# A two-layer decoder on one NeuronCore: first weights are loaded during the layer norm, an attention block's opening is reordered, and its last denominators and outputs are made in another way

## The reference

```python
x = x + L0_attn(_layernorm(x), ...)            # 16 heads of 64, keys: the 1024 tokens
x = x + L0_xattn(_layernorm(x), ctx_768, ...)  # 16 heads of 64, keys: 6404 context rows of 96
x = x + L0_ffn(_layernorm(x), ...)             # 8 experts, top 2, and a shared MLP; 512 hidden, gelu
x = x + L1_attn(_layernorm(x), ...)            # 16 heads of 8, rotary
x = x + L1_xattn(_layernorm(x), ctx_768, ...)  # 8 heads of 64, 6404 context rows
x = x + L1_ffn(_layernorm(x), ...)             # 8 experts, top 2, 512 hidden, relu

# one cross attention
sim  = jnp.einsum('bhid,bhjd->bhij', q, k) * SCALE
attn = jax.nn.softmax(sim, axis=-1)
out  = jnp.einsum('bhij,bhjd->bhid', attn, v)   # then heads side by side @ Wo + bo
```

## Time and profile before

| | |
|---|---|
| median of 3 runs | 4294.48 us (4294.39 to 4295.44) |
| the profiled execution's own time | 4298.41 us |
| its span, first to last instruction | 4296.6 us |
| mean granted TensorE clock, share of full | 0.961 |
| busy share of the span | PE 94%, PEld 50%, DVE 62%, ACT 42%, POOL 66% |
| DMA | 23.92 MB, mean 6 GB/s |
| L404, POOL's adds in c0 and c1 | x1176, 2482.9 us busy |
| L569, DVE's maxima in c0 and c1 | x1156, 1391.5 us busy |
| L473, ACT's exponentials in c0 and c1 | x1224, 1192.9 us busy |
| L785, PE's products in c0 and c1 | x4896 (two records each), 1179.9 us busy |

### The profile page before, as it was taken

How to read it: one execution, slowest core, us unless ns; L and a number is a source line. 1 busy time by engine, 2 the same in 40 slices (tenths; PEclk the granted TensorE clock), 3 DMA queues, 4 the chain that set the end, 5 groups by cost and what they waited for, 6 DMA issues and landing times. The chain is left out here.

```text
span 4296.6 us, 71788 instructions
## 1 busy us (share of the span) xinstructions
PE 4020.1 (94%) x26404; PEld 2141.9 (50%) x26404; DVE 2685.1 (62%) x3375; ACT 1813.3 (42%) x2105; POOL 2825.2 (66%) x1350
## 2 busy tenths in 40 slices
PE   6999699999999999999999997889899999999969
PEld 3444355554545555555555544633355554555537
DVE  5766767667676676766667622387666666667432
ACT  2444144444444444444444442256244444444433
POOL 3667187878887787877878891000077888878940
PEclk9999899999999999999999998989599999999979
DMA  1000000000000000000000000100000000000001
GB/s 36 6 6 2 5 2 2 2 2 2 2 2 3 2 2 2 2 3 2 2 1 1 2 1 27 35 1 1 4 2 2 2 2 2 2 1 2 1 13 32
DMA packets 25454, 23.92 MB, mean 6 GB/s; under 512 B 6321, under 2 KB 19106, under 8 KB 25122
## 3 DMA queue, kind: packets, MB, share of 16 engines
q1 hardware_dynamic: 23666, 17.05, 1.4%
q10 hardware_dynamic: 1456, 2.46, 0.2%
HBM read 18.97 MB, written 0.52 MB: 5 GB/s over the span
## 5 line engine op out<-in xcount | busy, mean ns | idle before, releaser
L404 POOL TENSOR_TENSOR c_SUM<-c_SUM,c_PR 128x896 f32<-128x896 f32 (+1 forms) x1176 | 2482.9, 2111 | 452.6 <-ACT c_PR L473 360.3
L569 DVE TENSOR_REDUCE c_MX<-c_XB 128x2 f32<-128x1024 f32 (+2 forms) x1156 | 1391.5, 1204 | 849.5 <-PE c_XB L735 848.9
L473 ACT ACTIVATE c_PR<-c_S 128x1024 f32<-128x1024 f32 (+1 forms) x1224 | 1192.9, 1023 | 1628.6 <-PE c_S L769 1553.0
L785 PE MATMUL c_O<-c_PR,c_V 128*64 128x512 f32 (+1 forms) x4896 | 1179.9, 600 | 1.3 <-ACT c_PR L473 1.3
L785 PEld LDWEIGHTS c_O<-c_PR,c_V 128*64 128x64 f32 (+1 forms) x4896 | 316.4, 136 | 542.2 <-issue 382.4
L769 PE MATMUL c_S<-c_SH,c_ONE 64*128 64x512 f32 x2448 | 486.4, 392 | 0.0
L735 PE MATMUL c_XB<-c_KHM,c_QH 64*128 64x512 f32 x1632 | 371.8, 449 | 26.4 <-DVE c_MX L569 20.2
L769 PE MATMUL c_S<-c_QH,c_KHM 64*128 64x512 f32 x1728 | 350.2, 401 | 0.1
L769 PE MATMUL c_S<-c_QH,c_KLM 64*128 64x512 f32 x1728 | 346.0, 396 | 0.0
L769 PE MATMUL c_S<-c_QL,c_KHM 64*128 64x512 f32 x1728 | 345.9, 395 | 0.0
L735 PEld LDWEIGHTS c_XB<-c_KHM,c_QH 64*128 64x128 f32 x1632 | 155.5, 186 | 378.8 <-DVE c_MX L569 206.7
(11 more groups left out here) (264 smaller groups left out, 4541.4 us busy)
## 6 DMA issues: line engine op xcount, KB each, us to landing
f_W<-in_L_w SPq DMA_DIRECT2D x34, 256.0 KB, 2.7
CTX<-in_ctx ACTq DMA_DIRECT2D x12, 192.0 KB, 4.4
c_WQ<-in_L_xattn_Wq SPq DMA_DIRECT2D x12, 64.0 KB, 1.9
c_WO<-in_L_xattn_Wo SPq DMA_DIRECT2D x12, 64.0 KB, 1.9
c_WK<-in_L_xattn_Wk SPq DMA_DIRECT2D x12, 48.0 KB, 1.8
c_WV<-in_L_xattn_Wv SPq DMA_DIRECT2D x12, 48.0 KB, 1.8
X<-in_x SPq DMA_DIRECT2D x1, 512.0 KB, 6.4
a_WQ<-in_L_attn_Wq SPq DMA_DIRECT2D x8, 64.0 KB, 1.9
```

The source lines that it names most:

```text
L404: pool.tensor_tensor(out[0:kp], out[0:kp], tile[0:kp], ALU.add).then_inc(summed, 1)
L473: act.activation(PR[0:kp, u % BUFS, :, :].rearrange("p h q -> p (h q)"), S[u % 2][0:kp, :], ACT.Exp)\
L569: dve.tensor_reduce(MX[:, q:q + tiles, :, column], bank[:].rearrange("p (h k) -> p h k", h=2) [:, :, 0:tiles * m].rearrange("p h (q k) -> ...
L785: last = pe.matmul(O[ROWS[h], :], V[pair.par][0:kp, t, ROWS[h]], PR[0:kp, u % BUFS, h, :], start=t == 0, stop=t == TILES - 1)
```

## The change

Four things are changed.

- **Loads.** `attention` and `experts` get the norm as an argument and call it themselves, ahead of their own block. The norm's SP issues the stage's first loads (`load_first`, `begin`): in attention WQ, WK, bias, WV, WO, in experts all that stood at the block's start. The norm uses banks and buffers of the stage. DVE's and PE's waits for POOL's fills move to the job M and to the first scores.
- **Lead.** K of chunk 0 is made in the bank O, so it doesn't wait for Q. Q of half 1 comes after chunk 2 (chunk 0 in a0), V of each chunk after the chunk's own maxima.
- **Last half.** POOL's and DVE's sums stop at tile `tail` (48 in c0 and c1, 6 in a0). PE adds the last tiles (three; two in a0) to SIDE itself, as `ones` times PR (`add_tile`), and then SUM to the same bank. In the wide case the split of the last half is 400 columns to POOL and 112 to DVE, not 448 and 64.
- **Last outputs.** Inverting, scaling, the output product and the addition to X go by quarters of 128 queries, the products in four banks of S.

```diff
+        self.tail = 2 * self.pairs_of_tiles - 2
+        self.last_split = HALF - 112 if wide else HALF
...
-        LEAD = [("side", ("Q", 0)), ("side", ("K", 0)), ("side", ("Q", 1)), ("V", 0)]
+        LEAD = [("side", ("Q", 0)), ("side", ("K", 0))]
         for c in range(CHUNKS):
             mine = [("max", i) for i, unit in enumerate(plan.maxima[0]) if unit[2] == c]
             LEAD += mine[:2]
             if c + 1 < CHUNKS:
                 LEAD += [("side", ("K", c + 1))]
-            LEAD += mine[2:]
-            if c + 1 < CHUNKS:
-                LEAD += [("V", c + 1)]
+            LEAD += mine[2:] + [("V", c)]
+            if c == (2 if plan.wide else 0):
+                LEAD += [("side", ("Q", 1))]
...
+        def load_first(sp):
+            load_q(sp, 0)
+            load_k(sp, 0)
+            sp.dma_start(BIAS[:], bias.partition_broadcast(P)).then_inc(bias_in, 16)
+            load_v(sp, 0)
+            load_o(sp, 0)
+
+        norm((O, SIDE), PR[:, 0, :, :].rearrange("p h (t d) -> p (h t) d", d=D), load_first)
...
                     for half in range(2):
-                        for t in range(TILES):
-                            add(pair, half, t)
+                        last = end and half == 1
+                        for t in range(plan.tail if last else TILES):
+                            add(pair, half, t, plan.last_split if last else SPLIT)
...
-                dve.wait_ge(filled, FILLS)
                 for kind, job in LEAD:
...
-                dve.reciprocal(RDEN[:], SIDE[:]).then_inc(side_free, 1)
-                dve.wait_ge(side_free, n + 1)
+                invert(0)
+                invert(1)
                 dve.wait_ge(evac, 2 * pairs)
-                dve.tensor_tensor(OT[:], OT[:], RDEN[:], ALU.mult).then_inc(normal, 1)
-                dve.wait_ge(side_done, n + 2)
-                output(1, n + 1)
+                scale_by(0)
+                invert(2)
+                scale_by(1)
+                add_output(0)
+                invert(3)
+                scale_by(2)
+                add_output(1)
+                scale_by(3)
+                add_output(2)
+                add_output(3)
...
+                def add_tile(t):
+
+                    kp = plan.tile_keys(t)
+                    if t == plan.tail:
+                        pe.wait_ge(side_free, plan.final_job(pairs, 0))
+                    for h in range(2):
+                        pe.matmul(SIDE[ROWS[h], :], ones[0:kp, ROWS[h]], PR[0:kp, (TILES + t) % BUFS, h, :],
+                                  start=t == plan.tail, stop=False)
...
                     pe.wait_ge(p_done, plan.step(pair.p, half, t) + 1)
+                    if plan.wide and half and isinstance(pair.p, int) and pair.p == pairs - 1 and t >= plan.tail:
+                        add_tile(t)
...
-                pe.wait_ge(filled, FILLS)
...
-                pe.wait_ge(summed, plan.added(pairs - 1, 1, TILES - 1))
+                if not plan.wide:
+                    for t in range(plan.tail, TILES):
+                        add_tile(t)
+                pe.wait_ge(summed, plan.added(pairs - 1, 1, plan.tail - 1))
                 if plan.wide:
-                    pe.wait_ge(reduced, plan.reduced(pairs - 1, 1, "all"))
-                pe.wait_ge(evac, 2 * pairs)
-                denominators(1).then_inc(side_done, 1)
+                    pe.wait_ge(reduced, plan.reduced_at_end(pairs - 1))
+                denominators(1, True).then_inc(side_done, 1)
                 pe.wait_ge(wo_in, 16 * pairs)
-                pe.wait_ge(normal, 2 * pairs)
-                pe.wait_ge(side_free, n + 1)
-                outputs().then_inc(side_done, 1)
+                for t in range(4):
+                    pe.wait_ge(normal, 2 * pairs + t)
+                    in_columns(last_bank(t), OT[:, t * P:(t + 1) * P], WO[:]).then_inc(side_done, 1)
```

More of the change, by code:

```diff
@@ L172, in over_pairs, with attention @@
     period(pair_at(pairs - 1), True)
-def attention(nc, held, name, pairs, keys, X, ident, w, bias, xt, src=None, C=P, src_in=None, scale=0.125):
+def attention(nc, held, name, pairs, keys, X, ident, w, bias, xt, src=None, C=P, src_in=None, scale=0.125, norm=None):
     plan = Schedule(keys)
@@ L625, in period @@
                             maxima(0)
-                            if plan.wide and group:
-                                sum_of_two(pair, half, group - 1)
+                            last = end and half == 1
+                            if plan.wide and group and not (last and 2 * group > plan.tail):
+                                sum_of_two(pair, half, group - 1, last)
                             if after == 1:
@@ L694, in side @@
                     last = None
-                    if pair is not None or n:
+                    if side_bank(pair, job) is SIDE and (pair is not None or n):
                         pe.wait_ge(side_free, n)
@@ L705, in side @@
                         pe.wait_ge(wk_in, 16 * (to.p + 1))
[L706 removed]
+                        last = in_columns(side_bank(pair, job)[:, 0:m], WK[0:C, :], src[0:C, c * CHUNK:c * CHUNK + m])
                     elif kind == "V":
@@ L875, in layer_norm, with _ @@
         with nc.Block() as block:
-            if load is not None:
-                @block.sync
-                def _(sp):
-                    for dst, dram in load:
-                        sp.dma_start(dst, dram).then_inc(sems.loaded, 16)
+            @block.sync
+            def _(sp):
+                for dst, dram in load or []:
+                    sp.dma_start(dst, dram).then_inc(sems.loaded, 16)
+                if begin is not None:
+                    begin(sp)
             @block.vector
```

193 lines of the change are left out of this document (107 added, 86 removed).

## The result

| | before | changed |
|---|---|---|
| median | 4294.96 us (4294.39 to 4298.17, 4 runs) | 4265.14 us (4260.11 to 4266.36, 4 runs) |
| profiled execution, span | 4298.41, 4296.6 | 4266.36, 4264.6 |
| mean granted clock | 0.961 | 0.965 |
| busy: PE, DVE, POOL | 94%, 62%, 66% | 95%, 64%, 65% |

The ratio is 0.992, with an interval of 0.9908 to 0.9932: faster by 0.8%, 30 us. The forecast was 4245.5, and 4265.14 lies above the range of 4232 to 4258.

What follows compares the result with a forecast made beforehand. TensorE, busy 94%, was taken to bound the bulk, with waits where stages meet. Gains of 14.4, 8.5 and 26.0 summed to 48.9 us, taking the profiled 4298.41 to 4249.5, forecast as a 4245.5 median; range 4232 to 4258.

Steps and rivals of the forecast that it cites:

- What bounds: PE, busy 94% of the span, bounds the bulk; where stages meet, the wait that ends last, at starts WQ's transfer.
- part 1: Stage starts: first loads issued under the norm shorten the gap from XT to PE, gaining 14.4 us over five stages.
- The crossing: Stage starts: PE's entry into the new block, the gap left after XT, taken as 0.4 us, bounds 0.2 to 1.5.
- Part 2, the start: Leads: K no longer waits for SIDE, so DVE's first maximum comes 6.05 us after PE's start instead of 11.13.
- Part 2, the clock: Leads: c0's stays at the full clock, c1's at the half; the lead part gains 8.5 us in all.
- before, the chain Q, V was spent at that clock in any case, now the first chunk is: Lead start at the half clock: one chunk takes 6.1 us for 5.1, so 1.0 us is given back.
- both leads at the full clock: Rival: leads of c0 and c1 both get the full clock, total 4233.5 us; chance 0.25.
- Parts 3 and 4: Last halves of c0 and c1 and a0's end: shorter POOL sums, tiles added on PE, quarters; 26.0 us gained.
- the estimate of 0.5 us against them: Last outputs: fixed latency of 0.06 us on each of nine added DVE instructions would cost 0.5 us an attention.
- the change touches none of that bulk: Whole kernel: the edit affects only where stages meet, not TensorE's bulk of the work; 0 forecast for unedited pieces.
- The rival "slower": Main loops: 49 us of their work moved to the half clock would cancel the gain; chance 0.02.
- DVE's wider reductions hold POOL: Last halves: one way POOL still paces them, twice 4 us less gain, 4253.5 us; that rival's chance 0.08.

Runs made afterwards that it cites:

- combined: Changed kernel plus norm_work's five products, the old lead order, and TWOS and FIVES behind the other tiles as in sums_last: 4239.06 us, 0.9841 of before.
- sums_last: Changed kernel with only the two grown tiles TWOS and FIVES allocated behind the attention's other tiles: 4264.47 us, 0.9906 of before.
- norm_work: Changed kernel with five fp32 products put on PE in each norm but the first, ahead of the transposes: 4240.86 us, 0.9855 of before.
- before_norm_work: Kernel before the change with only five fp32 products put on PE in each norm but the first: 4316.09 us, 1.0021 of before.
- lead_work: The combined kernel with one more fp32 product ahead of each V in the leads of c0 and c1: 4239.29 us, 0.9836 of before.
- a1_dense: Changed kernel with three more fp32 products on PE at the end of a1's lead: 4267.1 us, 0.9922 of before.
- a1_dense_later: The combined kernel with three fp32 products in a1 ahead of the second side job, two groups into its main loop: 4233.16 us, 0.9828 of before.

## Why the prediction was wrong

- **What bounds, and part 1: right.** WQ's transfer ended last at the starts; 14.7 us for 14.4. The crossing is 0.30 to 0.45 us for 0.4. The credit was given wholly to the norm; 4.5 us of it come without issuing under the norm, from WQ's place in the list together with the moved wait for the fills.
- **Part 2, the start: right.** The first maximum comes 6.00 us after PE's start for 6.05.
- **Part 2, the clock: wrong.** The first step that failed is "before, the chain Q, V was spent at that clock in any case, now the first chunk is": 1.0 us was charged for one chunk. PE stayed at the half clock for three chunks and the second Q, to 470.0, with 6.1 for 5.1 us a chunk, and Q at 2.0 on PE's own path instead of 0.6. These come to 3.4 us more than was charged; of the 6.65 for c0 2.1 came. In c1 the same case gave 10.8 for 4.65, since its lead now keeps the full clock from 26 us on: for this lead the rival "both leads at the full clock" came true. The two errors cancel, to 1.6 us more gain than forecast, and that is luck. What was wrong in both is that the clock of a lead seen in one trace was carried over to a lead that begins elsewhere and with other instructions.
- **Parts 3 and 4: right.** 12.6 and 12.3 for 12.3 each, 2.0 for 1.4. POOL's tiles took 2.05 us for 2.04. The quarters gave 1.25 us (5.64 for 6.89) where 0.8 was forecast, so a fixed latency of the added instructions didn't show; the estimate of 0.5 us against them took one figure for all nine, though six of them read PSUM.
- **A slip of the sum.** Both leads at the full clock come to 4233.2 by the prediction's own terms, not 4233.5; nothing hangs on it.
- **The sum: wrong by what was not in it.** This is the step that put the time outside the range: "the change touches none of that bulk" was true of the instructions and false of the time, and the forecast had no term for the unedited stages. a1 lost 11.3 us by 37 us more at the half clock, the loops 9.0, together 20.3 for 0. The rival "slower" named this very mechanism and looked for it in the loops alone, as something that would have to eat the whole gain; a1, with its sparse lead, was looked at nowhere. It should have been a width of the range: over the kernels that leave a1's instructions alone the loops and a1 together came to 2 us less (`combined`) up to 28 us more (`sums_last`) than in the kernel before.
- **The loops' 6 us from addresses** had no term. The prediction's rival that DVE's wider reductions hold POOL was about the last half; that a tile grown for the last half moves the others in all halves was not thought of.
- **The rule of the clock** in the Trainium skill, TensorE: Matmul & The Clock Gate, is that idle gaps bring the half clock back (section on HAM oscillation) and busy work releases it (Part 1). It agrees with `norm_work` (Q at 1.08 us), `before_norm_work` (1.98 behind a gap of 4.40) and `lead_work` (full clock at 9.37 of 10 us busy). a1 does not fit it: PE was busy 19.3 of 20 us and held at 0.50, and there the measurement decides.

What stays open is which of c0's and a1's cases an execution gets, and why addresses cost PE 0.2%.

## What to carry to other kernels

Where TensorE falls between two clock levels, an edit's price is its own work plus what its shift does to the stages behind it; put the second into the range even where nothing is edited, and read every stage's granted clock first, the sparse ones above all. A stage's opening can be worth more than its microseconds: when PE has no gap there, a few dense products in a phase in which it is idle anyway keep the full clock across the boundary (24 to 28 us here, over half of it in a1), and with the gap left in they bring nothing. A buffer that grows moves its neighbours; put it last.

## What was unexpected in the hardware

- PE stayed at 0.50 while busy 19.3 of 20 us, mostly on scores with 32 rows and products with 32 columns, and rose inside 4.48 and 4.04 us of fp32 products of 128 rows by 128 columns (`a1_dense`, `a1_dense_later`).
- The same a1 took 265 to 284 us in kernels that don't touch it, and in the changed kernel's family the low times go with work on PE in the norms.
- 4.1 KB a partition more in front of the other tiles cost about 0.3 of 129.4 us in each half, with the same instructions.
